# Recommendation model on one core: the sparse rows of the first eight tiles fetched one at a time by SP

## What is computed

```python
mask = seq_inputs[:, :, 0] != 0
other_info = jnp.concatenate([dense_inputs] + [emb_sparse[i][sparse_inputs[:, i]] for i in range(NS)], axis=-1)
seq_embed = jnp.concatenate([emb_seq[i][seq_inputs[:, :, i]] for i in range(NB)], axis=-1)
item_embed = jnp.concatenate([emb_seq[i][item_inputs[:, i]] for i in range(NB)], axis=-1)
...
h = jax.nn.sigmoid(info @ att_W1 + att_b1)
h = jax.nn.sigmoid(h @ att_W2 + att_b2)
logits = (h @ att_Wf + att_bf)[..., 0]
...
user_info = jnp.einsum('bl,bld->bd', att, seq_embed)
info_all = jnp.concatenate([user_info, item_embed, other_info], axis=-1)
info_all = bn_gamma * (info_all - bn_mean) * jax.lax.rsqrt(bn_var + BN_EPS) + bn_beta
info_all = prelu(info_all @ ffn_W1 + ffn_b1, ffn_a1)
info_all = prelu(info_all @ ffn_W2 + ffn_b2, ffn_a2)
return jax.nn.sigmoid(info_all @ out_W + out_b)
```

## Time and profile before

| | |
|---|---|
| runs | 1718.82, 1719.14, 1720.24 us (median 1719.14) |
| profiled execution, first to last instruction (span) | 1718.7 us |
| busy POOL / PE / DVE / ACT | 1285.4 / 956.0 / 476.8 / 421.1 us |
| indirect transfers issued by POOL | 1360 |
| transfers issued by SP | 48 (47 at the start, 1 at the end) |

### The profile page before, as it was taken

One profiled execution on the slowest core, in us unless ns is written; L12 is line 12 of the kernel. 1 busy time (PEld: TensorE's weight loads), 2 busy tenths in 40 slices (PEclk: granted clock), 3 DMA queues, 4 the chain that ended last, 5 costly groups with the idle time before them and its releaser, 6 DMA issues.

```text
span 1718.7 us, 11717 instructions
## 1 busy us (share of the span) xinstructions
PE 956.0 (56%) x2832; PEld 439.9 (26%) x2832; DVE 476.8 (28%) x1351; ACT 421.1 (24%) x770; POOL 1285.4 (75%) x1364
## 2 busy tenths in 40 slices
PE   1554656546564555646556464654646555464567
PEld 0222322222222222222222222322223222222222
DVE  1141322414133141322314132141322314132242
ACT  1131232213222131222213123221222213122222
POOL 6777777777777777777777777777777777777775
PEclk9656666566666656666566666656666565666655
DMA  3111111111111111111111111111111111111122
GB/s 50 28 26 26 27 27 27 26 26 27 27 27 26 26 27 26 27 26 26 27 26 27 26 26 27 26 27 26 26 27 26 27 26 27 27 26 27 26 26 19
DMA packets 56142, 46.22 MB, mean 27 GB/s; under 512 B 34209, under 2 KB 34337, under 8 KB 56097
## 3 DMA queue, kind: packets, MB, share of 16 engines
q0 software_dynamic: 43520, 44.65, 14.9%
q1 hardware_dynamic: 12578, 1.18, 0.5%
HBM read 45.74 MB, written 0.01 MB: 27 GB/s over the span
## 4 chain that ended last, share of the span: by engine, by line
POOL 54%; issue 26%; DMA 18%; POOLq 0%; PE 0%; DVE 0%; ACT 0%; SPq 0%; DVEq 0%; ACTq 0%
POOL hist L268 50%; DMA hist<-in_L_rec_emb_seq_dram,idx 18%; POOL sparse_rows L268 3%; POOL items L268 2%; DMA sparse_rows<-in_L_rec_emb_sparse_dram,idx_sparse 0%; POOLq L289 0%; DMA raw<-in_r_item_inputs_dram 0%; POOLq L60 0%; PE pre L410 0%; POOLq L288 0%; PE pre L416 0%; PE pre L411 0%; PE logits L422 0%; ACT x_sparse L446 0%; POOLq L271 0%
## 5 line engine op out<-in xcount | busy, mean ns | idle before, releaser
L268 POOL DMA_INDIRECT hist<-in_L_rec_emb_seq_dram,idx x1280 | 1208.7, 944 | 390.1 <-issue 351.1
L319 PE MATMUL turned<-ident,hist 128*128 128x128 f32 x640 | 176.0, 431 | 479.8 <-POOLq L289 424.1
L632 DVE TENSOR_TENSOR prod_t<-turned,item_t 128x512 f32<-128x512 f32 x160 | 110.6, 691 | 772.3 <-ACT hist_t L457 772.3
L325 PE MATMUL pre<-hist_t,w_hist 128*80 128x512 f32 x320 | 296.0, 1026 | 32.4 <-ACT hist_t L457 32.4
L319 PEld LDWEIGHTS turned<-ident,hist 128*128 128x128 f32 x640 | 122.7, 227 | 556.6 <-POOLq L289 474.0
L327 PE MATMUL pre<-prod_t,w_raw 128*80 128x512 f32 x320 | 255.1, 894 | 0.0
L457 ACT COPY hist_t<-turned 128x512 f32<-128x512 f32 x160 | 93.7, 586 | 567.8 <-PE turned L319 567.8
L462 ACT ACTIVATE hidden<-pre 80x512 f32<-80x512 f32 x160 | 94.6, 591 | 422.5 <-DVE pre L640 422.5
L640 DVE TENSOR_TENSOR pre<-pre,item_part 80x512 f32<-80x512 f32 x160 | 111.2, 695 | 236.0 <-PE pre L327 236.0
L687 DVE SCALAR_TENSOR_TENSOR sums<-hist,weight,sums 128x128 f32<-128x128 f32 x576 | 156.6, 347 | 0.0
L341 PEld LDWEIGHTS logits<-wf,hidden 128*128 128x128 f32 x640 | 110.3, 227 | 161.6 <-ACT hidden L467 92.7
(11 more groups left out here) (91 smaller groups left out, 416.2 us busy)
## 6 DMA issues: line engine op xcount, KB each, us to landing
hist<-in_L_rec_emb_seq_dram,idx POOLq DMA_INDIRECT x1280, 2.4
sparse_rows<-in_L_rec_emb_sparse_dram,idx_sparse POOLq DMA_INDIRECT x48, 3.3
raw<-in_r_seq_inputs_dram SPq DMA_DIRECT2D x1, 600.0 KB, 5.1
items<-in_L_rec_emb_seq_dram,idx POOLq DMA_INDIRECT x32, 3.4
w_raw<-in_L_rec_att_W_dram SPq DMA_DIRECT2D x1, 160.0 KB
fw<-in_L_rec_ffn_W_dram SPq DMA_DIRECT2D x3, 40.0 KB
ident<-identity_dram SPq DMA_DIRECT2D x1, 64.0 KB, 1.8
dense_rows<-in_r_dense_inputs_dram SPq DMA_DIRECT2D x1, 64.0 KB
```

Source lines behind the costliest of these rows:

```text
L268: gp.indirect_dma_start(rows, None, table, bass.IndirectOffsetOnAxis(ap=index, axis=0)).then_inc(landed, 16)
L319: last = nc.tensor.transpose(turned[g % 2][:, j * P:(j + 1) * P], hist[:, half, step * D:(step + 1) * D], ident[:, :])
L325: nc.tensor.matmul(pre1[g % 2][0:A1, :], w1_hist[:, :], hist_t[:, g % 2, :], start=True, stop=False)
L632: nc.vector.tensor_tensor(prod_t[:, slot, :].rearrange("p (l b) -> p l b", b=P), turned[slot][:, :].rearrange("p (l b) -> p l b", b=P), it ...
```

## The change

SP fetches the sparse rows of tiles 0 to 7 (pairs 0 to 3). After its 47 loads, it waits for the row numbers. It loops over the 128 partitions ("lanes"); in a pass it reads the 24 row numbers of that partition from `idx_sparse` into registers, eight in one load, and issues 24 transfers, each of one row of 256 bytes as two pieces of 128 bytes, into a buffer `landing` in DRAM. When all 768 transfers of a pair of tiles have landed, one further transfer brings that pair from `landing` to `sparse_rows`. GpSimd's sparse gathers begin at tile 8, and PE's wait for pairs 0 to 3 is for the one transfer.

```diff
+    ROW_PAIRS = 4
+    ROW_TILES = 2 * ROW_PAIRS
+    HALF = E // 2
+    BATCH = 8
...
+    landing = nc.dram_tensor("sparse_landing", (P, ROW_TILES * NS, 2, E), F32).ap()
...
+        rows_fetched = [sem(f"rows_fetched{p}") for p in range(ROW_PAIRS)]
...
+            sp.wait_ge(sparse_idx_ready, 1)
+            taken = [sp.alloc_register(f"row_number{i}") for i in range(BATCH)]
+            halves = sparse_table.rearrange("v (h e) -> v h e", h=2)
+            numbers = idx_sparse[0:1, :, :].rearrange("p t n -> p (t n)")
+            with nc.allow_non_contiguous_dma(reason="two halves of a row"):
+                with sp.Fori(0, P) as lane:
+                    for first in range(0, ROW_TILES * NS, BATCH):
+                        sp.load(taken, bass.at_runtime_partition(numbers[:, first:first + BATCH], lane))
+                        for i in range(BATCH):
+                            row = sp.snap(taken[i], min_val=0, max_val=NS * V - 1)
+                            slot = first + i
+                            sp.dma_start(landing[bass.ds(lane, 1), slot, :, 0:HALF], halves[bass.ds(row, 1), :, :])\
+                                .then_inc(rows_fetched[slot // (2 * NS)], 16)
+                for p in range(ROW_PAIRS):
+                    sp.wait_ge(rows_fetched[p], 16 * P * 2 * NS)
+                    sp.dma_start(sparse_rows[:, 2 * p:2 * p + 2, :].rearrange("p t (n h e) -> p (t n) h e", n=NS, h=2),
+                                 landing[:, 2 * NS * p:2 * NS * (p + 1), :, 0:HALF]).then_inc(sparse_landed[p], 16)
+
             sp.wait_ge(score_ready, PAIRS)
...
-            for tile in range(TILES):
+            for tile in range(ROW_TILES, TILES):
...
-                pe.wait_ge(sparse_landed[p], 2 * 16 * NS)
+                pe.wait_ge(sparse_landed[p], 16 if p < ROW_PAIRS else 2 * 16 * NS)
```

## The result

The changed kernel takes **3293.16 us** (median of 4 runs, 3292.77 to 3296.78) against 1719.34 us for the kernel before (1718.82 to 1720.24): ratio 1.9156 [1.9129, 1.9183]. The forecast was 1712.1, with a range from 1707 to 2110. The profiled execution took 3293.04 us, its span is 3291.2, so that 1.8 us lie outside it.

What follows compares the result with a forecast made beforehand. GpSimd's gathers bound the kernel, then the closing chain: 1718.7 - 7.0 = 1711.7, plus 0.4 makes 1712.1, range 1707 to 2110. A row on SP, 0.31 + 0.10 + 0.06 + 0.03 = 0.50 us, fits the limit of 0.529.

Steps and rivals of the forecast that it cites:

- The gain to be had: At the end of the kernel: 24 gathers removed save 7.0 us, not 30, because the closing chain becomes late next.
- rival C: Row transfers delay GpSimd's gathers on the shared DMA engines: 1719, chance 0.06, or about 1735, chance 0.05.
- 10 to 15 thousand: On SP's queue: the number of additional DMA packets expected, hidden as long as they spread or pipeline.
- The stage of 48.2 us: The closing stage, from pair 0's start on PE to the end of the kernel: 48.2 us.
- the deadline: SP's loop must end by 1656.7 for pair 0 to be ready at 1663.5, allowing 0.529 us a row.
- 87.9 + 3072p: The kernel's time in us if p, SP's time for each row, is over 0.529.
- 5.0 and a landing of 1.8: After SP's loop: 1.8 us for the last row to land, 5.0 for the first copy from `landing`.
- Two pieces: 0.31: On SP's queue: the issue of one row transfer in two pieces costs 0.31 us.
- rival A: Transfers with register-held DRAM addresses take SP's slower form, + 0.16 instead of + 0.03 a row: 2023, chance 0.26.
- register instructions and gaps: On SP's queue: source and destination offsets take two register instructions of 0.05, 0.10 us a row, bounds 0.04 and 0.12.
- load of eight: On SP's queue: one load of eight row numbers takes 0.5 us, 0.06 a row, bounds 0.005 and 0.23.
- Rival B: The load fetches its eight numbers one by one: 2238, or 1839 at half the price; chance 0.12.

Runs made afterwards that it cites:

- e1: Changed kernel without the row loop; SP copies pairs 0 to 3 from fixed table rows in four transfers: 1713.22 us.
- e5: Changed kernel with each row sent in one piece straight into `sparse_rows`, lanes written out, only the source in a register, no `landing` copies: 1713.56 us.
- e2: Changed kernel with SP fetching only pairs 0 and 1 (1536 rows), twelve row numbers in one load: 1713.17 us.
- e3: Changed kernel with all 3072 row transfers written out at fixed addresses, no loop, loads or register instructions: 1897.02 us.
- e4: Changed kernel without the loads; loop and register-held addresses stay, row number worked out from the lane: 2890.28 us.
- e6: Kernel before the change with one line added, `nc.dge_precook = False`: 1720.88 us.
- e7: Changed kernel with each row moved whole, as 16 pieces of 16 bytes instead of two of 128: 2821.76 us.
- e9: e5 with the 24 row numbers of a lane in one load instead of three loads of eight: 1713.31 us.
- e8: Changed kernel with transfers written out, fixed destination, source in a register, eight row numbers loaded once and reused: 2160.43 us.
- e10: Against e5, SP fetches the first 16 history columns of the last tile and only pair 0's sparse columns: 1694.83 us.
- e11: As e10, but SP fetches the last tile's first 24 history columns and no sparse ones: 1714.09 us.

## Why the prediction was wrong, point by point

**What held.** The gain to be had, 7.0 us and not 30: e1 gives 6 to 7, with pair 7 at 1699.72 for a forecast 1700.0. The gathers end at 1673 and keep 1.25 us. In e5, where all 3072 row transfers fall beside them, the last one starts at 1672.28, so rival C has fallen. SP's queue moved 18496 packets more than before (31074 - 12578), where 10 to 15 thousand were set, without effect. The stage of 48.2 us and the deadline held too: with p = 1.044 the forecast's own 87.9 + 3072p gives 3295, 2 us from the 3293.16. The closeness is in part luck: the copy was ready 2.8 us after its issue, where 5.0 and a landing of 1.8 were set (4 us too much), and 1.8 us lie outside the span, where 0.4 was set (1.4 too little). Half the rows kept the same deadline in full (e2).

**The step that failed** is the first line under "What a row costs SP": "Two pieces: 0.31". It took the issue from one-element and eight-row loads into the tile buffer. The transfer in question goes from DRAM to DRAM, and its issue takes 0.544 with fixed addresses (e3) and 0.617 as it stands. The row that would have warned was there, the 0.60 of the 64-row loads, and I named it; but I tied it to registers, took 0.03 for it in the sum, and in rival A its excess over the slowest of the short ones (0.60 - 0.44 = 0.16) rather than the 0.60 itself. Priced so, p would have been 0.60 + 0.03 + 0.10 + 0.06 = 0.79 and the time 2515, on the right side and still short. Of the 0.54 us that the sum lacked, the issue makes 0.28, more than half. The register instructions and gaps make 0.17: they measured 0.27, over twice their upper bound of 0.12.

The other terms were all low too:

| us a row | forecast | measured | from |
|---|---|---|---|
| issue (forecast with the gap behind it) | 0.31 + 0.03 | 0.617 | L275; 0.544 fixed (e3), 0.07 registers |
| register instructions and gaps | 0.10 | 0.063 + 0.058 + 0.153 | L273, two MOVEs, gaps in the chain of waits |
| load of eight | 0.06 | 0.120 | 0.964 / 8 |
| loop, branch, address of the next load | under 0.01 | 0.033 | the rest of 25.06 us a lane |
| sum | 0.50 | 1.044 | |

The lane's 25.06 us are (3215.2 - 32.1) / 127, from the loop's register instruction. Two MOVEs come with each transfer that has a register on both sides (one with one, e5), and each instruction of the queue is followed by 0.03 to 0.05 us; "one or two fused register instructions" counted neither.

**Rival A** was right that these issues are long, with the wrong cause and price. Registers make 0.07 of the issue (0.612 in e4 against 0.544 in e3); the rest is there with fixed addresses too (e3), and it is some 0.3 a row rather than 0.16 (0.617 against 0.31, 0.544 against 0.26). Its cause is not shown; that it is what e6 switches is a guess. **Rival B**, a trip for each number, isn't borne out at 8 and 12 numbers (0.96, 0.93), though the load is twice what I took, and in part it is at 22 and 24 (1.92, 1.72). For each number the loads took from 0.07 us (0.537 / 8 in e7, 1.716 / 24 in e9) to 0.12 (0.964 / 8).

**The range** failed because every bound was drawn from a neighbouring row, and their sum (0.31 + 0.12 + 0.23 + 0.16 = 0.82; the prediction says 0.85) ends far below 1.044. With the issue at 0.60 + 0.03, and the upper bounds of 0.12 and 0.23, it would have reached 0.98, and still not 1.044. The stated range of times was narrower again: it ends at 2110, a row of 0.66, because rival B at its full price was left out; no run shows that 0.66, and the runs showed 1.044 in the changed kernel and 0.532 in e5. The chance of 0.51 stood on a margin of 0.03 us in a sum whose largest term no row showed.

## What to carry to other kernels

Moving work to an idle queue is priced per instruction times its count, against a deadline: read from the timeline when the consumer wants the data, divide, and ask whether every instruction of the sequence, register moves and gaps included, fits. Take the price of an issue only from a transfer of the same kind (both ends, shape): here the same row cost 0.225 us to issue straight into the tile buffer and 0.617 us as two pieces into DRAM. And spend the freed time where the bound engine stands ahead of the closing stage: SP's loop was worth 6 us on the sparse rows alone, and 24 when most of it went to history rows that the closing stage waits for.

## What the runs showed of the hardware, unexpected

- SP issued a one-row transfer straight into the tile buffer, its source in a register, in 0.225 us (e5), and one from DRAM to DRAM in 0.52 to 0.62 (e3 0.544, e4 0.612, e7 0.520, e8 0.566, changed kernel 0.617). With `nc.dge_precook = False` in the kernel before, the one-element load has 0.61 instead of 0.26 and the 128-row vector loads 0.60 instead of 0.43 (e6). No run shows whether the two have one cause.
- A DRAM to DRAM transfer in two pieces is issued more slowly than one in sixteen, 0.617 and 0.520, and loads between such transfers take 0.96 and 0.54 (e7). Cause open.
- A load of row numbers took 0.54 to 0.96 us for 8, 0.93 for 12, 1.92 for 22 and 1.72 for 24 (e7, e5 and after; e2; e10; e9 and e11), so not one law of the count: loads of 8 alone range that far with the transfers around them. The shortest of all loads was 0.52 (e7).
- 3072 written-out transfers with their register instructions did not lengthen the kernel: e5 and e9 are within 0.4 us of e1, which has none of them.
- 3072 small transfers beside 1336 gathers left the gathers' 1.25 us as they were (e5: the last gather starts at 1672.28; e3, with pieces written to DRAM: 1672.04). Sixteen pieces a row may disturb them a little: in e7's one run the last gather starts at 1675.17.
